# One DRAM write of query rotary rows in place of two, and eight query loads in place of four

## The chip, the cores and the metric

The kernel runs on one core of one Trainium2 chip. The metric is the device time of one execution in microseconds (us).

## The reference, cut to what matters

Sixteen samples of 256 rows and 128 columns pass through one transformer block: a modulated layer norm, attention, and a mixture of eight experts of which each row takes two.

```python
c_q = x @ W_DQ
Qc = (c_q @ W_UQ)...                 # 16 heads, 8 content columns each
Qr = rope((c_q @ W_QR)...)           # 16 heads, 4 rotary columns each
Kc = (c_kv @ W_UK)...
Kr = rope((x @ W_KR)[:, None, :, :]) # one set, shared by all heads
scores = einsum('bhqd,bhkd->bhqk', concat(Qc, Qr), concat(Kc, Kr))
weights = softmax(where(causal, clip(scores, -80, 80), -inf) / sqrt(12))
```

## The kernel before

Attention is done batch by batch (a batch is one sample, 16 of them), the experts after it. In the attention stage every engine runs the same loop `schedule(emit)` with i from -3 to 15. In step i, batch f = i + 2 is projected, batch v = i + 1 is loaded, the scores of batch a = i are formed, and the later stages (output projection, second norm, routing) treat batches i - 1 to i - 3.

Queries and keys are stacked for TensorE through DRAM. TensorE takes four heads at once, in four row groups that begin at partitions 0, 32, 64 and 96. A row group has ROWS = 24 rows: 8 content rows and 16 rotary rows. The rotary rotation is not finished before the scores: `rope` holds for each query row its product with the cosine (half c = 0) and with the sine (half c = 1), and the scores' product over 24 rows adds up all combinations. For that the eight rows (4 cosine, 4 sine) of the queries stand twice, against two different sets of key rows.

The queue of SyncE, named SPq in the profile, issues nearly all transfers of this stage, in program order. In step i it does this:

- `stack(kdram, ...)` for batch v: waits until the three writes of the keys have landed, then issues four loads stk<-kdram, one for each row group, 24 rows by 4 KB (96 KB) each
- `stack(qdram, ...)`: the same for the queries, stq<-qdram, after the three writes of the queries have landed
- `keys_out(f)`: kdram<-cont (128 rows of 1 KB), then two writes kdram<-rope, in each of which 8 rows of SBUF are spread over 16 heads (128 KB)
- `load_bc(a)`: bc<-modrow, 192 KB
- `queries_out(f)`: qdram<-cont (128 KB), then twice the same 64 by 2 rows of `rope`, qdram<-rope (128 KB each), into rows 8 to 15 and 16 to 23 of qdram
- in steps 4 to 7 a part of the down weights, dn<-down, 384 KB

TensorE begins the scores of a batch, `scores(a, 0)` at line 483, when both of its stacks have landed (semaphores stq_in and stk_in) and the exponentials of the batch before are done. The semaphores q_out and k_out count the landed writes; ACT (line 816 on) and DVE (line 1196 on) wait for those of two batches back before they overwrite `cont` and `rope`.

After the last step, SPq loads the rows of the first expert block, xb<-queue (line 397), once the rows of the first twelve batches have been scattered by POOL (line 1423), and TensorE begins the experts at line 569.

Of the kernel before, what the change touches and what calls it, by code (L numbers as in the profile page):

```python
# [30 lines left out]
B, S, D = 16, 256, 128  # L31
P = 128
T = S // P
H, DH, DR, DL = 16, 8, 4, 32
# [14 lines left out]
RG = 4  # L49
NQ = H // RG  # L50


ROWS = DH + 4 * DR
GROUP = 32
# [45 lines left out]
def adaln_kernel(nc, x, consts, wsmall, wmod, gup, down, out):  # L100
# [3 lines left out]

    queue = nc.dram_tensor("queue", [(DUMMY + 1) * P, PAYW], fp32).ap()
    ydram = nc.dram_tensor("ydram", [2 * NTOK, D], fp32).ap()
    qdram = nc.dram_tensor("qdram", [2, ROWS, RG, NQ, S], fp32).ap()
    kdram = nc.dram_tensor("kdram", [2, ROWS, RG, NQ, S], fp32).ap()
    modrow = nc.dram_tensor("modrow", [B, 4 * D], fp32).ap()

# [1 line left out]
    with ctx:  # L112
# [36 lines left out]
        stq = sb("stq", [P, 2, NQ, S])  # L149
# [60 lines left out]
        def need(eng, sm, value):  # L210

            if isinstance(value, int) and value <= 0:
                return
            eng.wait_ge(sm, value)
# [15 lines left out]
        def par(b):  # L230
            return b % 2

        def half(b):
            return b // 2
# [85 lines left out]
        def _(sp):  # L320
# [21 lines left out]
            def section(dram, f, first, rows):  # L342

                return dram[par(f)][first:first + rows].rearrange("r i j n -> (r i j) n")
# [11 lines left out]

            def queries_out(f):

                need(sp, stq_in[par(f)], half(f) * (DMA * RG))
                sp.dma_start(section(qdram, f, 0, DH), cont[:, par(f), 0, :]).then_inc(s["q_out"], DMA)  # L360
                for n in range(2):
                    rows = section(qdram, f, DH + 2 * DR * n, 2 * DR).rearrange("(c p) n -> p c n", c=2)
                    sp.dma_start(rows, rope[0:H * DR, par(f), :, :]).then_inc(s["q_out"], DMA)

            def stack(dram, dst, arrived, written, f):

# [6 lines left out]
            def emit(i, pre, front, vproj, attn, back, norm, route):  # L373
                g, f, v, a, r, u, q = batches(i)
                if vproj:
                    stack(kdram, stk, stk_in, "k_out", v)
                    stack(qdram, stq, stq_in, "q_out", v)
                if front:
                    keys_out(f)
                if attn and a < B - 1:  # L380
                    load_bc(a)
                if front:
                    queries_out(f)
                if 4 <= i < 8:
                    part = slice((i - 4) * (E // 4) * (3 * D), (i - 3) * (E // 4) * (3 * D))
                    sp.dma_start(dn[:, part], down[:, part]).then_inc(s["w_in"], DMA)
# [67 lines left out]
        def _(pe):  # L454
# [19 lines left out]
            def scores(a, j):  # L474

                if j == 0:
                    need(pe, stq_in[par(a)], (half(a) + 1) * (DMA * RG))
                    need(pe, stk_in[par(a)], (half(a) + 1) * (DMA * RG))
                need(pe, s["exp_done"], NQ * a + j)
                for kt in range(T):  # L480
                    for i in range(RG):
                        at_ = slice(GROUP * i, GROUP * i + ROWS)
                        last = mm(SC[:, i, kt * S:S + kt * P], stk[at_, par(a), j, kt * P:(kt + 1) * P],  # L483
                                  stq[at_, par(a), j, kt * P:S], start=True, stop=True)
                last.then_inc(s["sc_done"], 1)
# [234 lines left out]
        def _(act):  # L720
# [79 lines left out]
            def emit(i, pre, front, vproj, attn, back, norm, route):  # L800
                g, f, v, a, r, u, q = batches(i)
                if front:
                    if i == -2:
                        act.wait_ge(s["modt_ready"], 1)
                    need(act, s["xT_done"], f + 1)
                    need(act, s["v_done"], f - 1)
                    af(hT[:, par(f), :], FA[:, 0:S], ACT.Identity, scale=ca1T[:, col(f)], bias=saT[:, col(f)])\
                        .then_inc(s["hT_ready"], 1)
                if attn:
                    exps(a, 0)  # L810
                if pre:
                    normalise(g)
                if back:
                    copy_out(r)
                if attn:
                    exps(a, 1)
                if front:
                    need(act, s["cont_done"], f + 1)
                    need(act, s["q_out"], 3 * DMA * (f - 1))
                    need(act, s["k_out"], 3 * DMA * (f - 1))  # L820
                    af(cont[:, par(f), :, :].rearrange("p c n -> p (c n)"), FA[:, :], ACT.Copy)\
                        .then_inc(s["cont_ready"], 1)
                if route:
                    odds(q)
                if norm:
                    squares(u)
                if attn:
                    exps(a, 2)
                if vproj:
                    if i == -1:  # L830
                        act.wait_ge(s["z_va"], 2)
                    need(act, s["v_done"], v + 1)
                    need(act, s["pv_done"], NQ * v - NQ)
                    for hf in range(2):
                        cols = slice(hf * (H // 2) * VW, (hf + 1) * (H // 2) * VW)
                        dst = va[:, par(v), :, cols].rearrange("p t (h w) -> p t h w", w=VW)
                        last = af(dst[:, :, :, hf * HALF:hf * HALF + DH],
                                  FB[:, 0:S].rearrange("p (t f h v) -> p t f h v", t=T, f=2, v=DH)[:, :, hf], ACT.Copy)
                    last.then_inc(s["v_ready"], 1)
                if norm:  # L840
                    normed_in(u, FA)
                if a == B - 1:
                    act.wait_ge(s["w_in"], 5 * DMA)
                    act.wait_ge(s["z_wgu"], 1)
                    load_expert(0)
                    load_expert(1)
                    scaled(0)
                if back:
                    attended_in(r)
                if a == B - 1:  # L850
                    scaled(1)
                if attn:
                    exps(a, 3)
                if norm:
                    queue_rows(u)
# [32 lines left out]
        def _(dve):  # L888
# [276 lines left out]
            def emit(i, pre, front, vproj, attn, back, norm, route):  # L1165
                g, f, v, a, r, u, q = batches(i)
                if norm:
                    residual(u)
                if back:
                    clip(r, 3)  # L1170
                if norm:
                    second_stats(u)
                if route:
                    places(q)
                if norm:
                    centre(u)
                if route:
                    counts(q)
                if attn:
                    clip(a, 0)  # L1180
                if q == EARLY - 1:
                    first_counts()
                if norm:
                    modulate(u)
                if route:
                    margins(q)
                if front:
                    need(dve, s["rope_done"], f + 1)
                    need(dve, s["q_out"], 3 * DMA * (f - 1))
                    need(dve, s["k_out"], 3 * DMA * (f - 1))  # L1190
                    tt(rope[:, par(f), :, :], FB[0:RR, 0:S].rearrange("p (o n) -> p o n", o=1).to_broadcast([RR, 2, S]),
                       cst[0:RR, C_TRIG:C_TRIG + 2 * S].rearrange("p (c n) -> p c n", c=2), ALU.mult)\
                        .then_inc(s["rope_ready"], 1)
                if q == EARLY - 1:
                    first_blocks()
                if route:
                    own_places(q)
                if back:
                    sums(r)
                if q == EARLY - 1:  # L1200
                    block_ends()
                if route:
                    shares(q)
                if back:
                    attended(r)
                if q == EARLY - 1:
                    block_experts()
                if route:
                    weights(q)
                if attn:  # L1210
                    clip(a, 1)
                if q == EARLY - 1:
                    block_rows()
                if attn:
                    clip(a, 2)
                if q == EARLY - 1:
                    first_table()
                if norm:
                    choose(u)
                if i in STATS_AFTER:  # L1220
                    dve.wait_ge(s["x_in"], 3 * DMA)
                    stats(STATS_AFTER[i])
# [357 lines left out]
```

## Time and profile before

| | us |
|---|---|
| median of three runs | 431.17 (430.13 to 434.17) |
| the profiled execution, its own time | 430.95 |
| span of that execution | 429.1 |
| TensorE busy in the span | 364.4 (85%) |
| DVE / ACT / POOL busy | 300.9 / 267.9 / 226.8 |
| share of time in which the 16 DMA engines moved packets of the hardware queue | 44.5% |

The profile is of one execution. The attention stage lies between 20 and 240 us of the span, the experts between 240 and 400 us, the sum of their results after that. In SPq's rows the time is that of issuing, which also holds the time in which an issue can't go on.

### The profile page before, as it was taken

To read this page: it belongs to the slowest core of one execution; us is meant where nothing else is said; L and a number is where in the kernel's file an instruction comes from. 1 tells how busy PE (TensorE), PEld (TensorE's weight loads), DVE (VectorE), ACT (ScalarE), POOL (GpSimd) and SP (SyncE) were. 2 spreads that over 40 slices of the span, in tenths; PEclk is the share of its full clock that TensorE was granted. 3 is DMA by queue.
4 is the path that set the end of the run, shared out by engine and by line. 5 is a ranking of instruction groups with operands and counts; after the bars stand their busy time and mean duration, and the time that the engine had idled before them with its cause. 6 is when DMAs were issued, how large, how long until landed. Compare 5 with 4: busy or idle time off the path is not lost.

```text
span 429.1 us, 12082 instructions
## 1 busy us (share of the span) xinstructions
PE 364.4 (85%) x3951; PEld 296.8 (69%) x3951; DVE 300.9 (70%) x1017; ACT 267.9 (62%) x464; POOL 226.8 (53%) x301
## 2 busy tenths in 40 slices
PE   3615889999798999898899899999999999999162
PEld 1413567767465676665666699999999999999120
DVE  2422799999688899887978877875555555555157
ACT  2323778988687898886756876666666666664000
POOL 2110324677577688677565767777744444444200
PEclk9965999999899899999959999999999999999668
DMA  8955655667677766656661322234342222210297
GB/s 272 339 110 131 152 146 147 159 163 172 161 190 195 204 176 165 153 135 164 170 176 34 70 75 71 76 93 111 99 137 84 60 60 58 60 46 32 88 289 217
DMA packets 56462, 58.36 MB, mean 136 GB/s; under 512 B 7216, under 2 KB 50225, under 8 KB 56273
## 3 DMA queue, kind: packets, MB, share of 16 engines
q1 hardware_dynamic: 52080, 49.10, 44.5%
q0 software_dynamic: 4320, 8.50, 5.7%
q8 instruction: 33, 0.54, 0.6%
q14 instruction: 29, 0.23, 0.2%
HBM read 33.76 MB, written 24.26 MB: 135 GB/s over the span
## 4 chain that ended last, share of the span: by engine, by line
PE 41%; POOL 26%; issue 15%; DMA 8%; DVE 6%; SPq 2%; ACT 1%; POOLq 0%; DVEq 0%
PE SC L653 22%; POOL queue L1423 13%; PE OB L665 11%; POOL rstd L1400 3%; PE FA L569 2%; PE SC L483 2%; DMA kdram<-rope 2%; POOL rstd L1375 2%; DMA pt<-ydram 1%; POOL ve L1395 1%; POOL pl L1388 1%; POOL root L1403 1%; DMA wm<-wmod 1%; DVE pt L1331 1%; POOL wog L1381 1%
## 5 line engine op out<-in xcount | busy, mean ns | idle before, releaser
L729 ACT ACTIVATE pt<-SC 128x1536 f32<-128x1536 f32 x64 | 92.9, 1451 | 39.8 <-PE SC L483 39.8
L653 PE MATMUL SC<-xTs,wgu 128*128 128x128 f32 x852 | 107.2, 276 | 0.6 <-issue 0.6
L653 PEld LDWEIGHTS SC<-xTs,wgu 128*128 128x128 f32 x852 | 100.8, 192 | 0.9 <-issue 0.9
L1458 POOL DMA_INDIRECT ydram<-ysb,xb x71 | 69.4, 978 | 59.8 <-DVE ysb L1236 48.5
L957 DVE SCALAR_TENSOR_TENSOR pt<-pt,cst 128x1024 f32<-128x1024 f32 x64 | 78.2, 1222 | 17.1 <-ACT pt L729 17.0
L1423 POOL DMA_INDIRECT queue<-pl,dest x64 | 76.2, 1190 | 24.7 <-POOL pl L1413 12.4
L483 PE MATMUL SC<-stq,stk 24*128 24x256 f32 (+1 forms) x1024 | 64.0, 367 | 29.1 <-DMA stq<-qdram 24.8
L483 PEld LDWEIGHTS SC<-stq,stk 24*128 24x128 f32 x1024 | 49.1, 196 | 44.6 <-DMA stq<-qdram 28.1
L798 ACT ACTIVATE sg<-SC 128x384 f32<-128x384 f32 x71 | 34.8, 490 | 53.5 <-PE SC L653 53.3
L790 ACT ACTIVATE wgu<-gu,ws 128x704 f32 x71 | 62.6, 882 | 0.5 <-issue 0.4
L505 PE MATMUL OB<-pt,va 128*32 128x256 f32 (+1 forms) x1024 | 59.3, 352 | 2.6 <-DVE pt L959 2.6
L665 PE MATMUL OB<-dn,hidT 128*128 x426 | 59.4, 275 | 1.6 <-DVE ysb L1236 1.6
L1160 DVE COPY xTs<-FA 128x128 f32<-128x128 f32 x71 | 20.7, 291 | 52.2 <-PE FA L569 39.9
L665 PEld LDWEIGHTS OB<-dn,hidT 128*128 128x128 f32 x426 | 53.2, 192 | 2.0 <-issue 2.0
L505 PEld LDWEIGHTS OB<-pt,va 128*32 128x32 f32 x1024 | 28.0, 114 | 23.3 <-issue 6.0
L1230 DVE TENSOR_TENSOR hidT<-sg,SC 128x384 f32<-128x384 f32 x71 | 39.2, 553 | 2.5 <-ACT sg L798 2.5
L1352 POOL TENSOR_TENSOR rstd<-var,mhalf 128x8 f32<-128x8 f32 x4 | 7.6, 1906 | 50.8 <-DVE var L908 50.8
L959 DVE TENSOR_SCALAR pt<-pt 128x512 f32<-128x512 f32 x64 | 27.2, 425 | 0.0
L1236 DVE SCALAR_TENSOR_TENSOR ysb<-OB,xb,ysb 128x128 f32<-128x128 f32 x71 | 24.5, 345 | 2.5 <-PE OB L665 2.5
L1162 DVE TENSOR_SCALAR ysb<-xb 128x128 f32<-128x128 f32 x71 | 20.5, 289 | 0.0
L569 PE MATMUL FA<-cst,xb 128*128 128x128 f32 x71 | 19.5, 274 | 0.5 <-DMA xb<-queue 0.5
L1381 POOL TENSOR_TENSOR wog<-ws,bc 128x128 f32<-128x128 f32 x16 | 9.6, 598 | 18.3 <-DMA bc<-modrow 18.2
(167 smaller groups left out, 517.2 us busy)
## 6 DMA issues: line engine op xcount, KB each, us to landing
stk<-kdram SPq DMA_DIRECT2D x64, 96.0 KB
stq<-qdram SPq DMA_DIRECT2D x64, 96.0 KB
xb<-queue SPq DMA_DIRECT2D x71, 65.5 KB, 1.8
kdram<-rope SPq DMA_DIRECT2D x32, 128.0 KB
qdram<-rope SPq DMA_DIRECT2D x32, 128.0 KB
pt<-ydram SPq DMA_DIRECT2D x16, 256.0 KB, 4.9
bc<-modrow SPq DMA_DIRECT2D x16, 192.0 KB
gu<-gup SPq DMA_DIRECT2D x1, 2816.0 KB, 12.1
```

The source lines that it names most:

```text
L483: last = mm(SC[:, i, kt * S:S + kt * P], stk[at_, par(a), j, kt * P:(kt + 1) * P], stq[at_, par(a), j, kt * P:S], start=True, stop=True)
L505: last = mm(OB[VW * i:VW * i + VW, g * S + kt * P:(g + 1) * S], va[:, par(a), kt, n * VW:(n + 1) * VW], pt[:, j, i, kt * S:S + kt * P], st ...
L569: nc.tensor.transpose(XP[:, 0:P], xb[:, slot(b), 0:D], ident).then_inc(s["xt_done"], 1)
L653: last = mm(GUB[b % 2][:, n, c * P:(c + 1) * P], wgu[:, b % 2, n, c * P:(c + 1) * P], xTs[:, b % DEEP, :], start=True, stop=True)
L665: last = mm(YP[:, 0:D], hidT[:, b % DEEP, n * P:(n + 1) * P], dn[:, bass.ds(e * (3 * D) + n * D, D)], start=(n == 0), stop=(n == 2))
L729: af(pt[:, j, :, 0:S + P], SC[:, :, 0:S + P], ACT.Exp, scale=SCALE).then_inc(s["exp_done"], 1)
L790: af(wgu[:, b % 2, :, 0:HID], gu[:, bass.ds(expert(b) * (2 * HID), 2 * HID)].rearrange("p (n h) -> p n h", n=2), ACT.Copy, scale=ws[:, W_N ...
L798: af(sg[:, b % 2, :], GUB[b % 2][:, 0, 0:HW], ACT.Silu).then_inc(s["sg_ready"], 1)
L957: stt(out=diag, in0=diag, scalar=E_LO, in1=mask, op0=ALU.max, op1=ALU.min)
L1230: tt(hidT[:, b % DEEP, :], sg[:, b % 2, :], GUB[b % 2][:, 1, 0:HW], ALU.mult).then_inc(s["hid_ready"], 1)
L1423: G.indirect_dma_start(queue, bass.IndirectOffsetOnAxis(dest[:, par(q), n:n + 1], 0), pl[:, par(q), n // 2, n % 2, :], None).then_inc(scat ...
L1458: G.indirect_dma_start(ydram, bass.IndirectOffsetOnAxis(xb[:, slot(b), D + 1:D + 2].bitcast(u32), 0), ysb[:, slot(b), :], None, bounds_che ...
```

## The change

The queries' rotary rows are written once, so `qdram` has 16 rows for each head instead of 24. Each row group is filled by two loads: 16 rows (content and rotary), and once more the last 8 rows of qdram into rows 16 to 23 of the group. The bytes that are loaded stay the same, the bytes written shrink by 128 KB a batch. The counts of semaphores follow: two writes instead of three, eight loads instead of four.

```diff
-    qdram = nc.dram_tensor("qdram", [2, ROWS, RG, NQ, S], fp32).ap()
+    qdram = nc.dram_tensor("qdram", [2, DH + 2 * DR, RG, NQ, S], fp32).ap()
...
             def queries_out(f):
-                need(sp, stq_in[par(f)], half(f) * (DMA * RG))
+                need(sp, stq_in[par(f)], half(f) * (DMA * 2 * RG))
                 sp.dma_start(section(qdram, f, 0, DH), cont[:, par(f), 0, :]).then_inc(s["q_out"], DMA)
-                for n in range(2):
-                    rows = section(qdram, f, DH + 2 * DR * n, 2 * DR).rearrange("(c p) n -> p c n", c=2)
-                    sp.dma_start(rows, rope[0:H * DR, par(f), :, :]).then_inc(s["q_out"], DMA)
+                rows = section(qdram, f, DH, 2 * DR).rearrange("(c p) n -> p c n", c=2)
+                sp.dma_start(rows, rope[0:H * DR, par(f), :, :]).then_inc(s["q_out"], DMA)
+
+            def queries_in(v):
+                need(sp, s["q_out"], 2 * DMA * (v + 1))
+                need(sp, s["sc_done"], NQ * v - NQ)
+                for i in range(RG):
+                    group = GROUP * i
+                    sp.dma_start(stq[group:group + DH + 2 * DR, par(v), :, :], qdram[par(v)][:, i])\
+                      .then_inc(stq_in[par(v)], DMA)
+                    sp.dma_start(stq[group + DH + 2 * DR:group + ROWS, par(v), :, :], qdram[par(v)][DH:, i])\
+                      .then_inc(stq_in[par(v)], DMA)
...
-                    stack(qdram, stq, stq_in, "q_out", v)
+                    queries_in(v)
...
-                    need(pe, stq_in[par(a)], (half(a) + 1) * (DMA * RG))
+                    need(pe, stq_in[par(a)], (half(a) + 1) * (DMA * 2 * RG))
...
-                    need(act, s["q_out"], 3 * DMA * (f - 1))
+                    need(act, s["q_out"], 2 * DMA * (f - 1))
...
-                    need(dve, s["q_out"], 3 * DMA * (f - 1))
+                    need(dve, s["q_out"], 2 * DMA * (f - 1))
```

## Rows read from the trace of the kernel before

**Rows 1.** Waits of TensorE in 60 to 222 us: total, times, longest.

```profile
PE SC L483 <- DMA stq<-qdram: 12.7, 9, 2.9
```

**Rows 2.** Waits of SPq in 60 to 222 us, the same columns.

```profile
SPq L370 <- DMA qdram<-rope: 3.8, 7, 1.1
SPq L370 <- DMA kdram<-rope: 0.6, 2, 0.4
```

**Rows 3.** Timeline of SPq, one batch: start, duration, line, transfer, count.

```profile
156.97 1.52 SPq L370 DMA_DIRECT2D stq<-qdram  x4
158.59 0.35 SPq L350 DMA_DIRECT2D kdram<-cont  x1
158.98 1.50 SPq L355 DMA_DIRECT2D kdram<-rope  x2
160.58 1.97 SPq L340 DMA_DIRECT2D bc<-modrow  x1
162.59 2.84 SPq L360 DMA_DIRECT2D qdram<-cont  x1
165.48 1.28 SPq L363 DMA_DIRECT2D qdram<-rope  x2
167.05 1.61 SPq L370 DMA_DIRECT2D stk<-kdram  x4
169.81 1.52 SPq L370 DMA_DIRECT2D stq<-qdram  x4
```

**Rows 4.** Timeline of TensorE: the first scores of batches 3, 4, 11 and 15.

```profile
72.53 0.94 PE L483 MATMUL SC<-stq,stk 24*128 24x256 f32 x16
...
83.92 0.94 PE L483 MATMUL SC<-stq,stk 24*128 24x256 f32 x16
...
175.07 0.94 PE L483 MATMUL SC<-stq,stk 24*128 24x256 f32 x16 [1.45 <-DMA stq<-qdram]
...
226.90 1.00 PE L483 MATMUL SC<-stq,stk 24*128 24x256 f32 x16
```

**Rows 5.** One line's and one tile's instructions: issue time minimum/median/maximum in ns.

```profile
L370 SPq DMA_DIRECT2D stq<-qdram x64: 289/364/1343, 30.8 to 222.7; - x64
L363 SPq DMA_DIRECT2D qdram<-rope x32: 602/631/3032, 24.9 to 218.6; - x32
```

**Rows 6.** Timeline of SPq: batch 0, the query loads of batches 0, 3 and 15.

```profile
21.42 1.60 SPq L355 DMA_DIRECT2D kdram<-rope  x2
...
30.81 1.58 SPq L370 DMA_DIRECT2D stq<-qdram  x4
...
65.81 1.85 SPq L370 DMA_DIRECT2D stq<-qdram  x4
...
221.58 1.52 SPq L370 DMA_DIRECT2D stq<-qdram  x4
223.20 0.35 SPq L340 DMA_DIRECT2D bc<-modrow  x1
```

**Rows 7.** The chain of work that ended last, first batch: start, duration, piece.

```profile
22.34 6.86 DMA kdram<-rope
...
32.03 3.52 DMA stq<-qdram
```

**Rows 8.** Busy times by stretch, then clock, DMA share, GB/s.

```profile
157.00:161.00 4.00, 4.00 (x59) 2.86 (x61) 3.93 (x15) 3.49 (x7) 3.03 (x6) 1.00 0.67 195
163.00:166.00 3.00, 3.00 (x59) 2.00 (x56) 2.69 (x11) 2.84 (x5) 2.45 (x4) 1.00 0.52 117
166.00:168.30 2.30, 2.30 (x26) 1.93 (x24) 2.30 (x11) 2.27 (x6) 1.40 (x2) 1.00 0.81 212
```

**Rows 9.** Timeline of SPq, a batch with a load of the down weights.

```profile
128.37 0.60 SPq L386 DMA_DIRECT2D dn<-down  x1
```

## The prediction

> **What bounds the kernel now.** I looked first at what TensorE waits for in the attention stage. Its waits in the middle of it are nearly all one kind: the first scores of a batch wait for the queries' load, nine times, 12.7 us in total [rows 1]. Where it does not wait, a batch takes it less: between the first scores of batches 3 and 4, 11.4 us [rows 4]. Between those of batches 4 and 15 lie 143.0 us, 13.0 a batch [rows 4]. So since batch 4 the stage runs at the pace of whoever delivers the queries, and that pace is 1 to 1.5 us a batch slower than TensorE's own.
>
> The deliverer is SPq, and its timeline is the next view [rows 3]. From the first query load of one batch (156.97) to that of the next (169.81) are 12.84 us. The rows follow one another with 0.04 to 0.1 us between, but for one gap of 1.15 us ahead of the last row. SPq's waits say the same: 4.4 us in 162 [rows 2]. SPq never waits for a compute engine there; it is always in an issue, and what it still has to issue comes late because of what stands ahead. Not all of that is work: bc<-modrow takes 1.97 us here and 0.35 us when nothing is ahead of it [rows 3, 6], and qdram<-cont takes 2.84 us where kdram<-cont, of the same size, takes 0.35 [rows 3]. These two issues stand still for about 1.6 + 2.5 = 4.1 us until earlier transfers have drained.
>
> Which transfers? Inside the same batch the DMA engines are 67% busy while the loads run, only 52% while SPq stands in qdram<-cont, and 81% once it is released [rows 8]. A queue that is held up while the engines are half idle is held by a transfer that uses few of them: the two kdram<-rope, each of which reads eight rows of SBUF for 128 KB, are the only such ones. The first batch shows them alone: issued at 21.42, landed at 29.20 (22.34 + 6.86) [rows 6, 7], 7.8 us, though no load lies ahead of them. In the batch of [rows 3] the key loads, which wait for just these writes, begin 8.07 us after the first kdram<-rope. With loads ahead and with none, the landing comes the same time after the issue. I take it from this that the key writes' drain is tied to when they are issued.
>
> One batch of SPq is then: query loads (1.6 us to the next issue's start, the key content write 0.4), key rotary writes issued at +2.0; the issue of qdram<-cont is let go 6.45 us after that (165.43 less 158.98), at +8.5; two qdram<-rope to +9.8; key loads from +10.1 to +11.7; query loads when the query writes have landed, at +12.84, that is 3.05 us after the last of their issues [rows 3].
>
> **The change part by part.** *Four more loads.* An issue of a query load takes 0.364 us in the median [rows 5], 0.40 with the gap to the next. The trace has no load of 16 or 8 rows. The lower bound is the fastest issue seen on that line, 0.289, the upper one that of a qdram<-rope, 0.631 [rows 5]; kdram<-cont with 128 rows takes 0.35 [rows 3], so the number of rows doesn't seem to matter, and I take 0.40. Four more are 1.6 us (1.3 to 2.7). They stand on the path: behind them on SPq are kdram<-cont and both kdram<-rope, so the key writes begin at +3.6 instead of +2.0. By what the first batch shows they drain, and let go of qdram<-cont, 1.6 us later.
>
> *One write fewer.* Its issue saves 0.64 us between qdram<-cont and the key loads. Its bytes saved are 128 KB; the 2.3 us in which both rotary writes and the content write drained moved 212 GB/s [rows 8], and 128 KB at that rate are 0.6 us. So the last query write lands 0.65 us earlier by its issue, and up to 0.6 more by its drain.
>
> *Two gates for the next query loads.* Gate one, the query writes: +3.6 + 6.45 + 0.04 + 0.64 = +10.7, and then the landing, which takes 3.05 us with two rotary writes to drain; less the 0.6 of the one that is gone, 2.4: +13.1. If nothing of the 0.6 comes back, +13.7. Gate two, the keys: their loads can't begin before the key writes have landed, +3.6 + 7.8 = +11.4, and take 1.6 to 1.75 us: +13.1. Today gate two stands at +2.0 + 8.07 + 1.65 = +11.7 and doesn't bind; after the change it does, which is why the saved write can't pay the loads back. A batch is 13.1 us instead of 12.84 in the place of [rows 3].
>
> *The whole stage.* The first query loads of batch 0 and of batch 15 start at 30.81 and 221.58 [rows 6], 190.8 us for 15 batches. The first three are shorter today, (65.81 - 30.81) / 3 = 11.67 each [rows 6], which is just gate two (+11.7): there gate one comes earlier, and they get the whole shift. Four batches carry dn<-down, 0.60 us more of issue [rows 9] ahead of the key loads, of which some 0.3 fit ahead of gate two: 13.4. So 11 x 13.1 + 4 x 13.4 = 197.7: 6.9 us more.
>
> *The landing.* Today the loads land 3.5 us after the last issue began (32.03 to 35.55) [rows 7], 4.7 us after the first. With eight issues the last begins at +2.8 and is a third of the size; with 3.0 us it lands at +5.8, 1.1 us later. At batch 15 today's load has landed just ahead of the scores, which show no wait at 226.90 [rows 4]: 221.58 + 4.7 = 226.3, slack of 0.6 us. Net 0.5.
>
> *The rest.* The experts' start hangs on TensorE's last steps and on POOL's scatters, which run in the same loop. I take it that the delay passes on whole. The relaxed counts of q_out for ACT and DVE cost and give nothing: they wait for writes two batches old. The bytes loaded stay. Sum: +6.9 + 0.5 = +7.4 us on the execution of 430.95: 438.3; against the median of 431.17, 0.2 higher: 438.5.
>
> **A rule of the skill against the trace.** In this trace SPq issues nearly without a pause [rows 2, 3], and a 96 KB load costs it 0.364 us [rows 5], against the 0.46 us that 96 KB take at the 212 GB/s of [rows 8]. The Trainium skill, in "DMA: Bandwidth & Descriptors", section "Issuing engines are not separate DMA queues", says that the time to initiate a DMA is usually small relative to the DMA itself. By that rule the four issues would be free, and the result is the first or second rival below; this trace disagrees with it for this queue.
>
> **The rivals.** *Absorbed (same).* The key writes drain when the engines get to them, not when they are issued; the added 1.6 us comes out of the 4.1 us in which bc and qdram<-cont stand still. For it: that stall is there to take. Against it: 7.8 us in an empty queue against 8.07 in a full one. Gate two would stay at +11.7 and gate one at 12.84 less 0.64: with half of that kept, 15 x -0.1 to -0.3 us and +0.5 to 1.1 for the landing: 428 to 431, taken as 430.
>
> *Paid (faster).* As before, and the saved write shows in full at gate one: -0.64 in each of about 13 batches, less the later landing: -8.3 + 1.0 = -7.3, 424. TensorE could follow, since its own batch is 11.4 [rows 4]. For it: gate one binds today [rows 2]. The Trainium skill, same page, section "Why a DMA increments its semaphore by 16 and not by 1", has a 24-row load run on 12 DMA engines, a 16-row one on 16 and an 8-row one on 8. By that rule the fullest engines still get two rows of each group, so loads that land sooner are no help to this rival; no row here shows the engines of a load.
>
> *Dear issues (slower still).* Each added load costs 0.63 us to issue, as a qdram<-rope does: 2.7 us in place of 1.6, decisive from the point where gate two binds: 1.1 us more in each of 15 batches, 438.5 + 16.5 = 455; with half of it, 447.
>
> **How the numbers follow.** Forecast 0.58; absorbed 0.20; paid 0.15; dear issues 0.07. What a measurement can tell from no change is about 1%, 4.3 us. The forecast's own bounds: if the gates come 0.3 us earlier a batch, 434; 0.4 later, 444. The range takes in the absorbed case and leaves out the paid one and most of the dear one: 429.5 to 444.5. Slower by over 1% (above 435.5): most of the forecast and the dear case, 0.61; within 1%: 0.22, the absorbed case and the low end of the forecast; faster by over 1%: 0.17.
>
> **What would show it.** In SPq's timeline: eight stq<-qdram in about 3.2 us; bc<-modrow and qdram<-cont together as long as now (about 4.8 us), not 1.6 shorter; a batch of 13.1 us; waits of the key loads for kdram<-rope that today are 0.6 us in total, growing to several us. In TensorE's waits: stq<-qdram well above 12.7 us. If the two stalled issues shrink by 1.6 us and a batch stays at 12.8 or below, the tie of drain to issue was wrong. A fall in TensorE's granted clock through its longer waits would add to the time beyond this sum.

## The result and the profile after

The changed kernel takes 445.04 us (444.07 to 450.02), the kernel before beside it 430.65 us (428.52 to 434.17). The ratio is 1.035, interval 1.024 to 1.046: slower, as forecast, by about twice the forecast's 7.4 us and just outside its range.

The profiled execution has a span of 444.2 us, 15.1 more than before. SPq's timeline, one batch of the changed kernel, answers to [rows 3]:

```profile
166.78 0.31 SPq L370 DMA_DIRECT2D stq<-qdram  x1
167.13 0.31 SPq L372 DMA_DIRECT2D stq<-qdram  x1
...
169.24 0.31 SPq L372 DMA_DIRECT2D stq<-qdram  x1
169.65 0.68 SPq L350 DMA_DIRECT2D kdram<-cont  x1
170.37 1.41 SPq L355 DMA_DIRECT2D kdram<-rope  x2
171.88 1.83 SPq L340 DMA_DIRECT2D bc<-modrow  x1
173.76 3.19 SPq L360 DMA_DIRECT2D qdram<-cont  x1
176.99 0.63 SPq L362 DMA_DIRECT2D qdram<-rope  x1
178.53 1.55 SPq L380 DMA_DIRECT2D stk<-kdram  x4
180.48 0.31 SPq L370 DMA_DIRECT2D stq<-qdram  x1
...
236.66 0.31 SPq L370 DMA_DIRECT2D stq<-qdram  x1
```

From one batch's first query load (166.78) to the next (180.48) are 13.70 us, where before were 12.84. The eight loads stand for 2.87 us until kdram<-cont, where four stood for 1.62. The two issues that stand still behind the key writes are as long as ever: 1.83 + 3.19 = 5.02 us against 4.81. They have given back nothing of what the loads added; the means over 14 batches are 4.98 us in both kernels. Between the end of qdram<-cont (176.95) and the next query loads lie 3.53 us; before, 4.38.

The waits (total, times, longest) answer to [rows 1, 2]. SPq's are those in 60 to 222 us, TensorE's those in 60 to 238 us, since its stage ends later now:

```profile
SPq L380 <- DMA kdram<-rope: 5.4, 8, 1.1
SPq L370 <- DMA qdram<-rope: 3.1, 7, 0.7
```

```profile
PE SC L493 <- DMA stq<-qdram: 19.2, 10, 3.3
```

TensorE's wait was 12.7 us before, in either stretch; in 60 to 222 us it is now 15.9. SPq now waits for the landing of the key writes eight times, 5.4 us, where it was twice and 0.6. This is the second gate of the forecast, and it does bind. The last row of the timeline above is the first query load of batch 15. From the first one of batch 0, at 30.80, it is 205.9 us, against 190.8 before: 15.1 more, the whole difference of the spans. After it both kernels take the same: 444.2 - 236.66 = 207.5 and 429.1 - 221.58 = 207.5. TensorE's granted clock, 0.936 of full speed before and 0.927 now, leaves no mark on that.

### The profile page after: what moved, and what is told of

Same layout as the page of the kernel before. It is cut to its first block, busy times and chain, and to the rows that moved or that the text cites. A ratio compares the mean times of both kernels' runs of the same rounds, so it can differ in the third digit from the quotient of the medians.

```text
span 444.2 us, 12130 instructions
## 1 busy us (share of the span) xinstructions
PE 368.9 (83%) x3951; PEld 299.0 (67%) x3951; DVE 302.3 (68%) x1017; ACT 268.3 (60%) x464; POOL 227.6 (51%) x301
## 4 chain that ended last, share of the span: by engine, by line
PE 37%; POOL 25%; issue 17%; DMA 11%; SPq 6%; DVE 4%; POOLq 0%; ACT 0%; DVEq 0%
PE SC L663 22%; POOL queue L1433 12%; PE OB L675 10%; POOL rstd L1410 3%; DMA qdram<-rope 2%; PE FA L579 2%; POOL wog L1391 2%; POOL ve L1405 2%; DMA kdram<-rope 2%; DMA bc<-modrow 2%; POOL rstd L1385 1%; POOL root L1413 1%; POOL pl L1423 1%; DMA pt<-ydram 1%; DMA wm<-wmod 1%
## 5 line engine op out<-in xcount | busy, mean ns | idle before, releaser
L663 PE MATMUL SC<-xTs,wgu 128*128 128x128 f32 x852 | 108.5, 278 | 0.6 <-issue 0.6
L663 PEld LDWEIGHTS SC<-xTs,wgu 128*128 128x128 f32 x852 | 101.9, 194 | 0.9 <-issue 0.9
L493 PE MATMUL SC<-stq,stk 24*128 24x256 f32 (+1 forms) x1024 | 66.2, 377 | 39.3 <-DMA stq<-qdram 34.8
L967 DVE SCALAR_TENSOR_TENSOR pt<-pt,cst 128x1024 f32<-128x1024 f32 x64 | 78.2, 1222 | 18.8 <-ACT pt L739 18.7
L493 PEld LDWEIGHTS SC<-stq,stk 24*128 24x128 f32 x1024 | 50.7, 203 | 55.8 <-DMA stq<-qdram 38.4
L1433 POOL DMA_INDIRECT queue<-pl,dest x64 | 73.7, 1152 | 24.7 <-POOL pl L1423 12.4
L515 PE MATMUL OB<-pt,va 128*32 128x256 f32 (+1 forms) x1024 | 60.6, 358 | 2.0 <-DVE pt L969 2.0
L1391 POOL TENSOR_TENSOR wog<-ws,bc 128x128 f32<-128x128 f32 x16 | 11.2, 702 | 31.8 <-DMA bc<-modrow 31.7
L791 ACT ACTIVATE pl<-h,rstd 128x256 f32<-128x256 f32 x32 | 14.4, 501 | 10.6 <-DMA queue<-pl,dest 10.6
```

Of the source, the lines that this page charges most:

```text
L515: last = mm(OB[VW * i:VW * i + VW, g * S + kt * P:(g + 1) * S], va[:, par(a), kt, n * VW:(n + 1) * VW], pt[:, j, i, kt * S:S + kt * P], st ...
L663: last = mm(GUB[b % 2][:, n, c * P:(c + 1) * P], wgu[:, b % 2, n, c * P:(c + 1) * P], xTs[:, b % DEEP, :], start=True, stop=True)
L967: stt(out=diag, in0=diag, scalar=E_LO, in1=mask, op0=ALU.max, op1=ALU.min)
L1433: G.indirect_dma_start(queue, bass.IndirectOffsetOnAxis(dest[:, par(q), n:n + 1], 0), pl[:, par(q), n // 2, n % 2, :], None).then_inc(scat ...
```

## The experiments

Several runs are read by three stretches of SPq's batch, worked out from the starts and ends in SPq's timeline and averaged over 14 of them, from batch 1's first query load to batch 15's: (A) from the first query load to the first key rotary write; (B) from there until the issue of qdram<-cont ends, called the release; (C) from the release to the next batch's first query load. Their sum is the batch.

| kernel | A | B | C | batch, us |
|---|---|---|---|---|
| before | 2.16 | 6.61 | 4.02 | 12.79 |
| changed | 3.52 | 6.55 | 3.73 | 13.80 |
| changed, measured again | 3.60 | 6.49 | 3.67 | 13.75 |
| split loads, three writes | 3.57 | 6.73 | 4.05 | 14.35 |
| four loads, one rotary write | 2.44 | 6.39 | 3.50 | 12.33 |
| tiny transfers ahead of the key writes | 3.93 | 6.50 | 4.16 | 14.59 |
| tiny transfers behind them | 2.20 | 8.61 | 4.05 | 14.85 |
| added loads from ScalarE, early | 2.69 | 6.35 | 3.65 | 12.69 |

My theory was that of the forecast: SPq's issue time ahead of the key writes sets the batch. The rivals were that the added time comes from the loads' shape on the DMA engines, that it is absorbed in stalls, and that every issue costs wherever it stands. The first four runs shared a chip on which the kernel before takes 449.94 us. No trace of that kernel was taken there. In the traces of the four, 222 to 228 us lie behind batch 15's first query load, where both kernels have 207.5 on the first chip. So most of the extra time lies there, and the four runs are read by ratio, and by batch against the row "before" of the first chip. Times expected for them as about 431 plus something are compared as ratios to 431.

**The change in two halves.** Split loads alone:

```diff
+            def queries_in(v):
...
+                    sp.dma_start(stq[group:group + DH + 2 * DR, par(v), :, :], qdram[par(v)][0:DH + 2 * DR, i])\
+                      .then_inc(stq_in[par(v)], DMA)
+                    sp.dma_start(stq[group + DH + 2 * DR:group + ROWS, par(v), :, :], qdram[par(v)][DH + 2 * DR:, i])\
+                      .then_inc(stq_in[par(v)], DMA)
...
-                    stack(qdram, stq, stq_in, "q_out", v)
+                    queries_in(v)
```

> The kernel before with its three query writes, but with eight query loads (16 rows and 8 rows a row group) in place of four. Theory (issue time ahead of the key writes sets the batch): the four issues cost 0.35 us each as the changed kernel shows, so the key writes go out 1.4 us later and the query writes too; nothing is saved; 15 batches of +1.3 us and a later landing: 449 to 452 us, slower than the changed kernel. Rival 1 (the lost time of the changed kernel is that of the shape of the loads on the DMA engines, not of issuing): about the same here. Rival 2 (absorbed in the stalls of the modulation load and the query content write): 431 to 433.

Measured: 471.49 us, ratio 1.0445 (1.036 to 1.053), as the theory had it (1.042 to 1.049). One write alone, with the loads of before; from batch 2 on it leaves out a part of the scores:

```diff
-                for n in range(2):
+                for n in range(2 if f < 2 else 1):
```

> The kernel before with its four 24-row query loads, but from batch 2 on the queries' rotary rows are written once; rows 16 to 23 of each row group then hold those of batch 0 or 1, so the rotary part of the scores is left incomplete. Theory: one issue of 0.64 us and 128 KB less between the key writes and the next query loads; the gate of the query writes falls by 0.6 to 1.2 us, that of the key writes (11.7 us after the loads) stands, so a batch goes from 12.7 to about 12.0 us: 420 to 423 us. Rival (the removed write is hidden because the key writes bind): 429 to 431.

Measured: 444.50 us, ratio 0.9873 (0.9807 to 0.9938). So the loads cost 4.5% and the write gives back 1.3%. It gave less than I expected, 0.46 us a batch and not 0.7. In this run too SPq waits for the key writes before the key loads, 6.7 us in 60 to 222, nine times, where it was 0.6 before and is 0.2 with split loads and all three writes. So it is the missing query write that makes the second gate bind, without any added load, and that gate takes back a part of the saving. The two halves multiply to 1.031. The changed kernel, run again on another chip, shows just that:

> The changed kernel itself, so that its ratio stands on the same chip as the reordered ones. From the runs of its two halves, 1.0445 (split loads) and 0.9873 (one write), their product: 1.031. Measured first: 1.035.

Measured: 444.89 us, ratio 1.0309 (1.0223 to 1.0396).

**Issue time without bytes.** In the kernel before, one transfer of 16 rows by 8 bytes after each query load:

```diff
                     sp.dma_start(dst[GROUP * i:GROUP * i + ROWS, par(f), :, :], dram[par(f)][:, i])\
                       .then_inc(arrived[par(f)], DMA)
+                    if written == "q_out":
+                        n = RG * f + i
+                        sp.dma_start(tiny[:, 2 * n:2 * n + 2], consts[0:16, 2 * n:2 * n + 2]).then_inc(s["tiny_in"], DMA)
```

> The kernel before, and after each of the four query loads of a batch one transfer of 16 rows by 8 bytes that nobody needs: issue time with next to no bytes, at the place of the added loads. Theory (issue time on SPq ahead of the key writes): 0.35 us each, 1.4 us a batch, as with the split loads: 449 to 452 us. Rival 1 (shape of the loads): no bytes, so within 2 us of 431. Rival 2 (absorbed): the same.

Measured: 474.46 us, ratio 1.0548 (1.0472 to 1.0624). Four transfers of 128 bytes cost more than the split of 384 KB of loads, and more than the 1.042 to 1.049 that I expected. Their issue takes 0.35 us in the median and the 24-row loads between them keep their 0.38, so A grows by 1.77 us. With split loads, where all eight take 0.31, it grows by 1.41. So issues alone are enough for a cost of this size; no bytes are needed. Absorption is out. Whether the shape of the loads adds something is left to the run with loads from ScalarE below.

The same four, issued right behind the two key rotary writes:

```diff
                     sp.dma_start(rows, src.to_broadcast([2 * DR, H, S])).then_inc(s["k_out"], DMA)
+                for n in range(RG * f, RG * f + RG):
+                    sp.dma_start(tiny[:, 2 * n:2 * n + 2], consts[0:16, 2 * n:2 * n + 2]).then_inc(s["tiny_in"], DMA)
```

> The kernel before with the same four tiny transfers a batch, but issued right after the two key rotary writes, ahead of the modulation load, where SPq stands still for 4 us anyway. Theory (the key writes' drain starts when they are issued and SPq then waits for it): the 1.4 us come out of the stall, 430 to 433 us. Rival (SPq is simply full, each issue costs its time wherever it stands): 449 to 452 us.

Measured: 478.34 us, ratio 1.0637 (1.0553 to 1.0721). Here my theory was wrong (it had 1.00) and its rival right, even exceeded (1.042 to 1.049). SPq's timeline of this run shows why:

```profile
61.24 1.47 SPq L356 DMA_DIRECT2D kdram<-rope  x2
63.15 5.13 SPq L358 DMA_DIRECT2D tiny<-consts  x4
68.33 0.43 SPq L341 DMA_DIRECT2D bc<-modrow  x1
68.81 0.43 SPq L363 DMA_DIRECT2D qdram<-cont  x1
69.28 1.28 SPq L366 DMA_DIRECT2D qdram<-rope  x2
```

The tiny transfers stand still, and bc<-modrow and qdram<-cont, which used to, take 0.43 us each. I call this standing still the hold. It does not belong to those two transfers, nor to their bytes. It falls on what comes next behind the key writes. It doesn't end earlier for what is put into it: here it lasts until 7.0 us after the key writes' issue. The 192 KB and 128 KB transfers, which used to stand in it, go out after it. So a stall of this queue was no room to put issues into. B grows by 2.0 us.

**Does the hold move with the order?** Key writes ahead of the query loads, in the kernel before:

```diff
                     stack(kdram, stk, stk_in, "k_out", v)
+                    if front:
+                        keys_out(f)
                     stack(qdram, stq, stq_in, "q_out", v)
-                if front:
+                elif front:
                     keys_out(f)
```

> The kernel before with one change of order on SPq: the three key writes of a batch are issued between the key loads and the query loads, not behind the query loads. Reading of the traces so far: the next two transfers behind the key rotary writes, whichever they are, are held until those have drained, 6.6 us after the first was issued; everything else takes its 0.3 to 0.7 us. Then the first two query loads stand for 4 us together, the modulation load and the query content write take 0.4 each, and a batch is 1.8 (key loads) + 0.4 + 6.6 + 0.8 + 0.4 + 0.4 + 1.3 = 11.7 us against 12.8, near TensorE's own: ratio 0.96 to 0.98. Rival (the hold belongs to the modulation load and the query content write, which wait for something of their own): the query loads take 1.6 us and the two still stand for 4 us; ratio 0.99 to 1.01.

Measured: 527.08 us, ratio 1.2171 (1.2053 to 1.229). And in the changed kernel:

> The changed kernel with the same order, key writes ahead of the query loads. By the same reading six of the eight query loads are issued after the hold, 2.1 us where the other kernel has 0.8, and one write of 0.68 less: 11.7 + 1.3 - 0.7 = 12.3 us a batch: ratio 0.97 to 0.99, 0.5 us a batch above the run with keys first. Rival: the added loads now fall into the hold and cost nothing: the same as keys first or 0.01 less.

Measured: 531.93 us, ratio 1.2316 (1.2212 to 1.242). The reading of the hold was right, the time far off. SPq's timeline of the first of the two, and its waits:

```profile
164.41 0.34 SPq L350 DMA_DIRECT2D kdram<-cont  x1
164.80 1.48 SPq L355 DMA_DIRECT2D kdram<-rope  x2
166.38 5.29 SPq L370 DMA_DIRECT2D stq<-qdram  x4
171.76 0.35 SPq L340 DMA_DIRECT2D bc<-modrow  x1
172.16 0.63 SPq L360 DMA_DIRECT2D qdram<-cont  x1
```

```profile
SPq L350 <- ACT cont L823: 108.4, 14, 9.5
```

The four query loads now take 5.29 us in place of 1.5, and the two transfers behind them are free. But kdram<-cont waits for ScalarE's copy to `cont`, 108.4 us in total, 14 times. That copy follows the scores of the present batch, and the query loads queued behind the wait are those of the next. I had left out this wait, since it is hidden in the old order. It closes a loop over scores, copy, key writes, hold and loads. A batch takes 18.8 us, and the two ratios say nothing on the smaller question of the added loads in the hold.

**Without the hold.** The keys' rotary rows, the same for all heads, are written for one row group and read four times:

```diff
+    krot = nc.dram_tensor("krot", [2, 4 * DR, NQ, S], fp32).ap()
...
-                    sp.dma_start(rows, src.to_broadcast([2 * DR, H, S])).then_inc(s["k_out"], DMA)
+                    sp.dma_start(rows, src.to_broadcast([2 * DR, NQ, S])).then_inc(s["k_out"], DMA)
...
+                    sp.dma_start(stk[group:group + DH, par(v), :, :], kdram[par(v)][:, i])\
+                      .then_inc(stk_in[par(v)], DMA)
+                    sp.dma_start(stk[group + DH:group + ROWS, par(v), :, :], krot[par(v)])\
+                      .then_inc(stk_in[par(v)], DMA)
```

> The kernel before with its query side as it was, but the rotary rows of the keys are written once for one row group (2 x 32 KB in place of 2 x 128 KB) and read by all four row groups, in eight key loads in place of four. Theory (SPq is held by the slow drain of the two key rotary writes: two transfers behind them can't be issued for 4 us): the hold is gone, a batch of SPq falls to 10 to 11 us although there are four issues more, and TensorE's own 11.4 to 12 us bind: ratio to before 0.95 to 0.98. Rival (four issues more cost 1.4 us a batch wherever they stand, and nothing is gained by smaller writes): 1.03 or more.

Measured: 414.74 us, ratio 0.9593 (0.9543 to 0.9642). With the change on top:

> The changed kernel with the same key side as the run with keys written once: one query rotary write, eight query loads, eight key loads. Theory: SPq has 2.8 us of query loads, 2.8 of key loads, about 3 of other issues and 2.5 of landing, about 11 us a batch, still no more than TensorE's own: within 1% of the run with keys written once, ratio to before 0.95 to 0.98; the change costs nothing where the key writes don't hold the queue. Rival (the cost of the split loads is in the loads themselves): 3% or more above the run with keys written once.

Measured: 412.85 us, ratio 0.9551 (0.9486 to 0.9615), the fastest kernel of the study. SPq's timeline of the first of these two, and the start of each batch's scores on TensorE:

```profile
157.04 1.49 SPq L356 DMA_DIRECT2D krot<-rope  x2
158.62 0.38 SPq L341 DMA_DIRECT2D bc<-modrow  x1
159.05 0.43 SPq L361 DMA_DIRECT2D qdram<-cont  x1
```

```profile
147.53 0.94 PE L495 MATMUL SC<-stq,stk 24*128 24x256 f32 x16
...
159.08 0.94 PE L495 MATMUL SC<-stq,stk 24*128 24x256 f32 x16
...
170.63 0.94 PE L495 MATMUL SC<-stq,stk 24*128 24x256 f32 x16
```

With 64 KB in place of 256 KB of key rotary writes nothing stands still behind them, and though SPq has four issues more, a batch takes 11.55 us, twice alike here, and TensorE waits for no load any more in 60 to 222 us. So it is TensorE's own pace. The whole change, eight query loads for four and one write for two, costs nothing there: the intervals of 0.959 and 0.955 overlap. The split of the loads alone was not run on this kernel, and where TensorE sets the pace a slower load could hide.

**Added loads from another queue.** The changed kernel with its four 8-row loads issued by ScalarE, ahead of the last exponentials of a batch:

```diff
-                    sp.dma_start(stq[group + DH + 2 * DR:group + ROWS, par(v), :, :], qdram[par(v)][DH:, i])\
-                      .then_inc(stq_in[par(v)], DMA)
...
+                if vproj:
+                    need(act, s["q_out"], 2 * DMA * (v + 1))
+                    for m in range(RG):
+                        lo = GROUP * m + DH + 2 * DR
+                        act.dma_start(stq[lo:lo + 2 * DR, par(v), :, :], qdram[par(v)][DH:, m])\
+                           .then_inc(stq_in[par(v)], DMA)
```

> The changed kernel, but the four added loads of 8 rows are issued by ScalarE, just ahead of the last exponentials of a batch; same bytes, same shapes, same count of transfers. Theory (what costs is SPq's issue time ahead of the key writes): SPq is as in the run with one write, ratio to before 0.985 to 1.00. Rival (number or shape of the loads on the DMA engines): 1.03, as the changed kernel. If ScalarE's waiting for the query writes holds its exponentials, TensorE's waits for them would show it, and the time lies between.

Measured: 516.63 us, ratio 1.1929 (1.1872 to 1.1986), worse than any case I had given, and of no use for the question, since the place in ScalarE's order could be the whole cause. So the same loads, right after the copy to `cont`:

> The changed kernel with the four added loads issued by ScalarE again, but a third of a batch earlier, right after the copy to cont instead of ahead of the last exponentials. With the late place a batch took 18.9 us, since the next scores waited for loads that ScalarE issued at the end of its step. If that was all of it: about 4 us earlier, 14 to 15 us a batch, ratio 1.03 to 1.07. If the loads themselves were slow from a second queue: 1.15 or more. If SPq's issue time is all that counts and ScalarE's stall is hidden: 0.985 to 1.00.

Measured: 431.35 us, ratio 0.9974 (0.9921 to 1.0026). The place was the cause: a third of a batch earlier takes 85 us off. And with SPq rid of four issues the changed kernel's whole loss is gone, with the same bytes, shapes and count of transfers. So the shape of the loads was not the cost. A falls from 3.6 to 2.69. A batch is still 0.36 us longer than with one write and four loads, though the two ratios' intervals touch. ScalarE's waits show what may be the price: idle time ahead of an instruction that follows its own issues, with no semaphore named. TensorE, which waited 15.9 us for loads in the changed kernel, waits 0.9 for them here, but 8.8 for ScalarE's exponentials. In 60 to 222 us:

```profile
ACT ex L761 <- issue: 12.0, 10, 3.0
```

```profile
PE SC L491 <- ACT pt L737: 8.8, 14, 1.1
PE SC L491 <- DMA stq<-qdram: 0.9, 2, 0.6
```

**The write: issue or bytes?** In the kernel before, the second rotary write of the queries replaced by a transfer of 128 bytes, with the same part of the scores left out:

> The kernel before, but from batch 2 on the second write of the query rotary rows is replaced by a transfer of 16 rows by 8 bytes that counts in its place: the issue stays (0.35 us in place of 0.64), the bytes go; the rotary part of the scores is left incomplete as in the run with one write. That run saved 0.46 us a batch. Theory (what the write costs is mostly its place in SPq's order): some 0.3 us a batch saved, 4 us, ratio to before about 0.990. Rival (it costs by its bytes on the DMA engines): the whole saving of the run with one write or more, ratio 0.987 or below. If neither counts: 1.00.

Measured: 426.56 us, ratio 0.991 (0.9868 to 0.9953). That is the 0.990 of the theory of the issue, but the interval also reaches the 0.987 of the theory of the bytes. The split between issue and bytes stays open.

## Why the forecast was right in its sign and wrong in its size

**Right.** *SPq is the bound* in the attention stage, and TensorE's own batch is 11.4 to 11.6 us: once the hold was gone a batch took 11.55. *The four loads stand on the path*: A grew by 1.36 us; I had said 1.6. An issue of 16 or 8 rows takes 0.31 us, not 0.36. In 2 of 16 batches kdram<-cont itself now stands still (0.68 and 0.91 us), which I had not foreseen. *The hold is tied to the key writes' issue*: B, forecast at 6.45 and unchanged, is 6.35 to 6.73 in every kernel of the table but the one with transfers put in between, with A anywhere between 2.2 and 3.9. *Gate two binds*: 5.4 us of waits. Of the signs I had named, a batch of 13.1 us did not come out, but 13.8. The others did: eight loads in 2.87 us, the two held issues as long as before, longer waits of TensorE.

**The step that failed** is gate one, "the landing, which takes 3.05 us with two rotary writes to drain; less the 0.6 of the one that is gone, 2.4: +13.1". By it C would fall to 3.05 us (+10.05 to +13.1), 1.3 less than in the batch of [rows 3]. Measured means: 4.02 before, 3.73 and 3.67 after, 0.3 us less. From the end of the write's issue to the next query loads are 2.92 us, where the forecast had 2.4. That is 0.5 us a batch, nearly all that is missing.

Two errors are in it. I took one batch as the base, whose landing of 3.05 us was long: the mean from the last query write's issue to the next query loads is 2.52 us before. And I subtracted the write twice, once by its issue (0.65) and once by its drain (0.6), as if the last write's landing only got shorter when one write is gone. The traces record the counts of the semaphores (some are missing, so I take medians of 14 batches), and so when the last query write has landed. It is 2.43 us after the end of the last issue before and 2.38 with split loads, both with two writes. With one write it is 2.41 with four loads, and 2.78 and 2.60 in the two runs of the changed kernel. So it gets no shorter, and with one write SPq also waits longer for the key writes, 0.79 us a batch against 0.32, before it can issue the key loads that stand ahead of the query loads. The forecast had another value beside it, +13.7 "if nothing of the 0.6 comes back". The measured batch is 13.8, but that value started from the one long batch, so it is near by luck.

Gate two was mis-sized too: forecast +13.05, measured (means of the same timeline) 3.52 + 6.55, then 0.81 for the rotary write and 0.79 of waiting, 11.67 until the key loads, and 1.75 for them: +13.4. So gate one's 13.1 could not have been reached in any case. I had the key writes land 7.8 us after their issue. By the counts of their semaphore (medians again) that is right for the kernel before, 7.80; one write has 7.77, added loads from ScalarE 7.71. In the changed kernel it is 8.13 in both runs, with split loads 8.22, with tiny transfers ahead 8.20. So with four more issues ahead the key writes also land some 0.3 us later after their own issue, a term that the forecast did not have. It is not shown that the added issues are the cause: the write without bytes has 8.03 with none added.

Together: 197.7 us forecast from the first to the last query loads, 205.9 measured, 0.55 us a batch, 8.2 in all. *The landing* term (+0.5 us) came out as nothing: both kernels end 207.5 us after batch 15's first query load. That all of it passes on to the end was right by the same numbers.

**The rivals.** Absorbed and paid both needed the stalled 4.1 us to give way; they went from 4.81 to 5.02 us, in the means not at all, and the run with tiny transfers behind the key writes shows that nothing put there is absorbed. The saved write is worth 1.3%, where "paid" had 1.7%. Dear issues was wrong in its cause, 0.31 us each and not 0.63; that half of it, 447 us, lies near the measured time is chance.

**The rule of the skill.** The Trainium skill, "DMA: Bandwidth & Descriptors", section "Issuing engines are not separate DMA queues", holds that issuing is usually small beside the DMA. For this kernel the runs decide against what follows from it, that four more issues would be free: four transfers of 128 bytes a batch cost 5.5%, and with four issues moved off SPq the ratio fell from 1.031 to 0.997. The same sentence says that initiating DMAs on several engines saves only the sequencer's time; the last ScalarE run agrees, and here that time was the whole loss.

**Open.** What the hold counts, descriptors, transfers or something else, was not tried; the runs show only that it falls on the transfers next behind the key writes, whatever their size, and that it goes when these are a quarter as large. Of C's 3.73 us in the changed kernel 0.81 are the write's issue, 0.79 the wait for the key writes, 1.75 the key loads, and 0.38 the wait for the query writes. Why a single query write takes as long to land as the last of two stays open, and so does whether issue or bytes make up the write's 1.3%.

## What to carry to other kernels

Count a serial queue like an engine: add its issues, find out what holds it, and take means over all batches, not one batch, as terms. A stall inside a queue need not be slack; here an issue put into it pushed what was there behind the release. And the cost of an edit belongs to the kernel around it: the change costs 3% while SPq binds and nothing once cheaper key writes let TensorE bind.

## What was not expected of the hardware

- Transfers of 16 rows by 8 bytes took 0.42 to 3.3 us to issue (median 1.05) behind the two key rotary writes, and 0.33 to 1.35 us (median 0.35) ahead of them.
- A load of 16 or 8 rows of 4 KB took 0.31 us to issue, one of 24 rows 0.36, a transfer of 16 rows by 8 bytes 0.35 (medians). The time of an issue doesn't follow the bytes.
- One query write of 128 KB took no less time to land after its issue than the second of two: 2.4 to 2.8 us against 2.4 (medians).
- The kernel before took 449.94 us on one chip and 430.65 to 432.69 on others; ratios of the changed kernel agree (1.035, 1.031, and 1.031 from its halves on the slow chip).
